# Query, key and value rows of two blocks made inside the first expert stage of a macaron transformer block

## What is computed

```python
x = L0_attn_batch                       # (16, 512, 128) fp32: 8192 rows of 128
x = x + 0.5 * ffn(layernorm(x))         # 8 experts, top 2 by router, sigmoid gates, plus a shared expert
x = x + attn(layernorm(x))              # per batch of 512 rows: q, k, v; softmax per tile of 128 keys;
                                        # the four tiles' results added and divided by their norms; Wo, bo
x = x + 0.5 * ffn(layernorm(x))
# an expert: (silu(g*x @ w_in[e]) * (g*x @ w_sw[e])) @ w_out[e], 128 -> 256 -> 128
```

## Time and profile before

| | us |
|---|---|
| median of three runs | 915.17 (913.69 to 920.29) |
| profiled execution: its time | 916.05 |
| profiled execution: span | 914.3 |
| stage 1, to about | 205 |
| experts(0), about | 205 to 392 |
| attention, about | 392 to 650 |
| experts(1) and the rest, about | 650 to 914 |

### The profile page before, as it was taken

One profiled execution on the slowest core, in us unless ns is written; L12 is line 12 of the kernel. 1 busy time (PEld: TensorE's weight loads), 2 busy tenths in 40 slices (PEclk: granted clock), 3 DMA queues, 4 the chain that ended last, 5 costly groups with the idle time before them and its releaser, 6 DMA issues.

```text
span 914.3 us, 19543 instructions
## 1 busy us (share of the span) xinstructions
PE 817.6 (89%) x5765; PEld 721.4 (79%) x5765; DVE 674.9 (74%) x2191; ACT 573.6 (63%) x1670; POOL 607.7 (66%) x689
## 2 busy tenths in 40 slices
PE   3696877679998999979999999998799999999998
PEld 3475666579998899945777777777599999999997
DVE  6787865746667888836888899897766667777765
ACT  3422432137776677679989899873267667766662
POOL 3888888877777777730466767667656667666670
PEclk9787978889999999989999999998899999999999
DMA  9711111434355555420011111111443345555433
GB/s 243 207 48 49 46 46 49 91 92 111 100 154 149 157 148 142 124 70 1 24 36 37 40 39 42 36 40 45 88 109 91 83 135 164 166 165 144 141 96 101
DMA packets 114091, 88.02 MB, mean 96 GB/s; under 512 B 14595, under 2 KB 103302, under 8 KB 113990
## 3 DMA queue, kind: packets, MB, share of 16 engines
q1 hardware_dynamic: 95840, 51.09, 22.1%
q0 software_dynamic: 17280, 35.69, 12.0%
q10 hardware_dynamic: 870, 0.01, 0.1%
HBM read 43.68 MB, written 43.04 MB: 95 GB/s over the span
## 4 chain that ended last, share of the span: by engine, by line
PE 50%; POOL 30%; issue 9%; DMA 5%; DVE 3%; ACT 2%; SPq 0%; DVEq 0%; POOLq 0%; ACTq 0%
POOL pairs L463 14%; POOL results L989 10%; PE bank L1119 9%; PE bank L1567 5%; PE bank L1591 5%; PE bank L1095 5%; PE bank L1096 5%; PE bank L1097 5%; POOL pairs L1222 3%; PE bank L1577 3%; POOL PAY L454 3%; PE bank L1104 2%; PE bank L1556 2%; PE bank L1544 2%; DMA Y<-results 1%
## 5 line engine op out<-in xcount | busy, mean ns | idle before, releaser
L989 POOL DMA_INDIRECT results<-YO,XS x142 | 149.9, 1056 | 77.7 <-ACT YO L1052 39.9
L1222 POOL DMA_INDIRECT pairs<-PAY,POS x128 | 137.0, 1071 | 75.8 <-DVE POS L259 37.9
L1095 PE MATMUL bank<-round_b,round_a 128*128 128x256 f32 x568 | 172.6, 304 | 11.7 <-DVE round_a L928 10.6
L989 POOL DMA_INDIRECT results<-XTR x142 | 147.1, 1036 | 49.3 <-issue 40.2
L934 DVE TENSOR_TENSOR big<-bank,big 128x512 f32<-128x512 f32 x158 | 109.1, 690 | 87.8 <-PE bank L1097 85.4
L1097 PE MATMUL bank<-round_b,round_a 128*128 128x256 f32 x568 | 161.0, 283 | 0.0
L1096 PE MATMUL bank<-round_b,round_a 128*128 128x256 f32 x568 | 160.9, 283 | 0.0
L463 POOL DMA_INDIRECT pairs<-PAY,POS x128 | 128.3, 1003 | 40.5 <-issue 19.7
L1119 PE MATMUL bank<-WOE,big 128*128 x1136 | 151.2, 276 | 0.1
L1060 ACT ACTIVATE big<-bank 128x512 f32<-128x512 f32 x158 | 94.7, 599 | 75.1 <-PE bank L1097 75.0
L1119 PEld LDWEIGHTS bank<-WOE,big 128*128 128x128 f32 x1136 | 139.1, 193 | 0.6 <-issue 0.5
(11 more groups left out here) (240 smaller groups left out, 1814.9 us busy)
## 6 DMA issues: line engine op xcount, KB each, us to landing
XTR<-pairs SPq DMA_DIRECT2D x71, 130.0 KB
XS<-pairs SPq DMA_DIRECT2D x71, 130.0 KB
Y<-results SPq DMA_DIRECT2D x64, 128.0 KB
YF<-results SPq DMA_DIRECT2D x64, 128.0 KB
pairs<-PAY,POS POOLq DMA_INDIRECT x256, 2.4
out<-X SPq DMA_DIRECT2D x16, 256.0 KB, 3.0
results<-XTR POOLq DMA_INDIRECT x142, 2.6
results<-YO,XS POOLq DMA_INDIRECT x142, 2.4
```

The costliest lines, as they stand in the source:

```text
L989: pool.indirect_dma_start(results, bass.IndirectOffsetOnAxis(ap=XS[:, u, j, AT_DEST:AT_DEST + 1].bitcast(U32), axis=0), YO[:, u, j, :], No ...
L1095: pe.matmul(ps, wl[:, w], hi, start=True, stop=False)
L1222: pool.indirect_dma_start(pairs, bass.IndirectOffsetOnAxis(ap=POS[:, b % AB, j, c:c + 1], axis=0), PAY[:, b % AB, c, j, :], None).then_inc ...
```

## The change

The list of experts(0) gets two entries (`PREPARED`, ahead of tiles 52 and 58) that are no tiles. At such an entry PE turns the normalised rows of block 0 or 1, ACT copies them to `AXT`, PE makes queries, keys and values in the banks that a tile would have used, and ACT takes them out to `QT`, `KT`, `V`. ACT makes the deviations of blocks 0 to 2 in one go in the step of tile 40, DVE the shifts in the step of tile 42, and ACT normalises half a block in each of the steps of tiles 44 to 47 (blocks 0, 1) and of tiles 61 and 62 (block 2). The attention stage leaves out these steps for these blocks. The buffers concerned are allocated before experts(0) instead of after it.

```diff
+    PRE = 2
+    NORMED = 3
+    NORMED_FROM = 44
+    PREPARED = (52, 58)
...
                 for i in range(NT):
+                    if not ffn and i in PREPARED:
+                        tile_at.append(None)
...
+                def nth(n):
+                    return past + n - prepared_to(n) + 1
+
+                normed_at = {} if ffn else {NORMED_FROM + 2 * b + h: (b, h) for b in range(PRE) for h in range(2)}
+                if not ffn:
+                    normed_at.update({PREPARED[-1] + 3 + h: (PRE, h) for h in range(2)})
...
+                    def shifts():
+                        dve.wait_ge(k["a_rstd"], NORMED)
+                        dve.scalar_tensor_tensor(out=NA[:, 0:NORMED, :], in0=MA[:, 0:NORMED, :, 0], scalar=-1.0,
+                                                 in1=RA[:, 0:NORMED, :], op0=ALU.mult, op1=ALU.mult)\
+                           .then_inc(k["a_shift"], NORMED)
...
+                            if not ffn and t == NORMED_FROM - 2:
+                                shifts()
...
+                    def deviations():
+                        act.preload_act_table_set("natural_log_exp_and_others")
+                        act.wait_ge(k["a_stats"], 2 * NORMED)
+                        act.activation(LA[:, 0:NORMED, :], MA[:, 0:NORMED, :, 1], ACT.Ln, bias=eps_c[:, :])\
+                           .then_inc(k["a_log"], NORMED)
+                        act.wait_ge(k["a_log"], NORMED)
+                        act.activation(RA[:, 0:NORMED, :], LA[:, 0:NORMED, :], ACT.Exp, scale=-0.5)\
+                           .then_inc(k["a_rstd"], NORMED)
+
+                    def normalise_half(b, h):
+                        act.wait_ge(k["a_shift"], NORMED)
+                        if b >= 2:
+                            act.wait_ge(k["a_turned"], b - 1)
+                        for j in range(2 * h, 2 * h + 2):
+                            ins = act.activation(AN[:, b % 2, j, :], X[:, BT * b + j, :], ACT.Identity,
+                                                 bias=NA[:, b % 4, j:j + 1], scale=RA[:, b % 4, j:j + 1])
...
+                    def rows_across(n):
+                        b = block_of(n)
+                        act.wait_ge(k["a_turned"], b + 1)
+                        act.activation(AXT[:, b, :], bank[2 + n % 2][:, :], ACT.Copy).then_inc(k["a_copied"], 1)
+
+                    def take_across(n):
+                        b = block_of(n)
+                        act.wait_ge(k["q_made"], b + 1)
+                        act.activation(QT[:, b, :], bank[2 + n % 2][:, :], ACT.Identity, bias=bq_s[:, :], scale=SCALE)\
+                           .then_inc(k["q_ready"], 1)
...
+                            if n >= 2 and is_prep(n - 2):
+                                pe.wait_ge(k["k_ready"] if g else k["q_ready"], prepared_to(n - 2))
...
+                    def turn_rows(n):
+                        b = block_of(n)
+                        pe.wait_ge(k["a_normed"], b + 1)
+                        pe.wait_ge(k["e_silu"], nth(n - 2))
+                        for j in range(BT):
+                            mm = pe.transpose(chunk(bank[2 + n % 2], j), AN[:, b, j, :], ident[:, :])
+                        mm.then_inc(k["a_turned"], 1)
+
+                    def make_rows(n):
+                        b = block_of(n)
+                        pe.wait_ge(k["a_copied"], b + 1)
+                        pe.matmul(bank[2 + n % 2][:, :], WT[:, 0, :], AXT[:, b, :], start=True, stop=True)\
+                          .then_inc(k["q_made"], 1)
+                        pe.wait_ge(k["e_hid"], nth(n - 2))
+                        pe.matmul(bank[4 + n % 2][:, :], WT[:, 1, :], AXT[:, b, :], start=True, stop=True)\
+                          .then_inc(k["k_made"], 1)
+                        pe.wait_ge(k["e_out"], tile_at[n - 2] + 1)
...
+                            if is_prep(i):
+                                turn_rows(i)
+                            else:
+                                up(i)
...
+                        if 0 <= i - 1 < ALL and is_prep(i - 1):
+                            make_rows(i - 1)
+                        elif 0 <= i - 1 < ALL:
                             down(i - 1)
...
-                    if 0 <= i + 3 < NB:
+                    if NORMED <= i + 3 < NB:
                         shift(i + 3)
...
-                    if 0 <= i + 2 < NB:
+                    if PRE <= i + 2 < NB:
                         turn(i + 2)
```

More of the change, by code:

```diff
@@ L862, in is_half, with is_prep, is_tile, prepared_to @@
                 def is_half(n):
-                    return tile_at[n] is None
+                    return ffn == 1 and tile_at[n] is None
+                def is_prep(n):
+                    return ffn == 0 and tile_at[n] is None
+                def is_tile(n):
+                    return tile_at[n] is not None
+                def prepared_to(n):
+                    return tile_at[:n + 1].count(None) if ffn == 0 else 0
+                def block_of(n):
+                    return prepared_to(n) - 1
+                def nth(n):
[3 more added lines that the diff above has]
+                    normed_at.update({PREPARED[-1] + 3 + h: (PRE, h) for h in range(2)})
+                    assert NORMED_FROM > sum_place(NORMED - 1) + 8 and NORMED_FROM + 2 * PRE < PREPARED[0]
                 def halves_to(n):
@@ L970, in _ @@
                                 dve_moments(dve, st, *halved_at[t])
-                        if i + 3 < ALL and not is_half(i + 3):
+                        if i + 3 < ALL and is_tile(i + 3):
                             no.ahead(tile_at[i + 3])
                         if i + 2 < ALL:
-                            low(i + 2)
-                            if i + 2 and not is_half(i + 2):
+                            if not is_prep(i + 2):
+                                low(i + 2)
+                            if i + 2 and is_tile(i + 2):
                                 weights(i + 2)
@@ L1064, in _ @@
                         if i + 2 < ALL:
-                            high(i + 2)
+                            if not is_prep(i + 2):
+                                high(i + 2)
                         elif ffn and i < ALL:
@@ L1069, in _ @@
                             scale(tile_at[i + 3], 1)
-                        if 0 <= i - 1 < ALL and not is_half(i - 1):
+                        if 0 <= i - 1 < ALL and is_tile(i - 1):
                             send(i - 1)
+                        elif 0 <= i - 1 < ALL and is_prep(i - 1):
+                            take_across(i - 1)
+                        if not ffn and 0 <= i < ALL and tile_at[i] == NORMED_FROM - 4:
+                            deviations()
+                        if 0 <= i < ALL and tile_at[i] in normed_at:
+                            normalise_half(*normed_at[tile_at[i]])
                 @block.tensor
@@ L1122, in down @@
                         mm.then_inc(k["e_down"], 1)
+                    def turn_rows(n):
[14 more added lines that the diff above has]
+                        pe.wait_ge(k["e_out"], tile_at[n - 2] + 1)
+                        pe.matmul(bank[6 + n % 2][:, :].rearrange("p (j d) -> p j d", d=D), ones[0:3, :],
+                                  bias3[:, 0:1, :].to_broadcast([3, BT, D]), start=True, stop=False)
+                        for j in range(BT):
+                            mm = pe.matmul(chunk(bank[6 + n % 2], j), AXT[:, b, j * P:(j + 1) * P], WT[:, 2, :],
+                                           start=False, stop=(j == BT - 1))
+                        mm.then_inc(k["v_made"], 1)
                     no.ahead(0)
```

92 lines of the change are left out of this document (51 added, 41 removed).

## The result

The changed kernel is slower: 923.65 us against 918.29 us (medians of 14 runs each, taken in turn), a ratio of 1.0075 with a 95% interval of 1.0057 to 1.0092, so 6.9 us (5.2 to 8.4); the two medians by themselves lie 5.4 apart.

The account below looks back on a forecast made before the run. TensorE was taken to bound the expert tiles, with POOL just as near the edge, and ACT attention's first blocks. Cost 5.3 + 0.3 = 5.6, gain 3.4 + 0.5 = 3.9: 1.7 us slower, 916.9 us from 915.17; range 909.5 to 921.5.

Parts of the forecast that it names:

- terms of the start: Start of attention: scores follow the last tile at once, maximum(0, 1) waits for Y of block 15; gain 3.4 us (3.2 to 4.2).
- the cost of the entries: Tiles 49 to 70: two entries add 7.14 us of TensorE, partly refilling 2.1 us of idling; 5.3 us taken (5.0 to 7.1).
- T at 399 or later: Sign of a wrong forecast: TensorE's last tile ends (T) at 399 us or later, not near 397; entries cost more than their matmuls.
- eight tiles: After an entry: POOL, needing 2.71 us a tile, fills its lag again within eight tiles (8 x 0.16 = 1.3 us).
- Cost 5.0 to 8.1: Bounds of the whole cost in the sum; with gain 2.9 to 5.7 they gave -0.7 to +5.2 us.
- Deviations and normalising: Tile 40's step and six half blocks: table loads 0.3 us (bounds 0 and 3.1), normalising nothing, 1 us if not.
- the cover named for it: Tile 40's step: DVE's 1.98 us wait for Y of block 5 leaves Silu idle 2.23 us, covering most of 3.1 us.
- After maximum(0, 1): Blocks 0 and 1 of attention: at most 1.5 us less work, 1 to 1.6 lost to half clock; gain 0.5 (-0.3 to 1.5).
- The start gives nothing back: Rival, start of attention: late Y of block 15 and half clock leave gain 2, cost 6 to 7.1; +4 to +5 us; chance 0.17.
- More is hidden: Rival, entries and start: entries refill more idle time, Y lands 1.2 us sooner, clock costs nothing; -2 to -4 us; chance 0.25.
- Table loads at each Identity: Rival, ACT in the expert stage: Silu's set lacks Identity, 14 us reach TensorE, some 930 us; chance 0.04.

Follow-up runs that it names:

- e2: Changed kernel with total and added of blocks 14 and 15 moved later in DVE's attention queue (i == 4 and 6): ratio 0.9925 to the kernel before.
- e1: Changed kernel with its second entry ahead of tile 60 instead of 58: ratio 1.0062 to the kernel before.
- e4: Changed kernel with ten extra useless 512-column matmuls on TensorE while it waits for exps(0, 1): ratio 1.0049 to the kernel before.
- e8: Changed kernel with every total(b) and what follows it one tile's step later in the first expert stage: ratio 0.9999 to the kernel before.
- e10: Kernel before, with every total(b) one tile's step later in its first expert stage: ratio 0.9967 to the kernel before.
- e12: Kernel before, totals one tile's step later in the first expert stage and the last totals late in attention: ratio 0.9931 to the kernel before.
- e9: Changed kernel, totals one tile's step later in the first expert stage and the last totals late in attention: ratio 0.9849 to the kernel before.

## Why the prediction was wrong, point by point

**The sign and most terms of the start were right.** The scores follow the last tile at once, Y of block 15 takes the place of the rows as the last thing, maximum(0, 1) comes 11.7 us after the last send instead of 15.2: a gain of 3.5 for the 3.4 forecast. e2 showed the mechanism.

**The step that failed is the cost of the entries**, "I take 5.3", bounded by "if none, 7.1". It measured 8.6 us (7.9 to 8.8 between any two of the executions at full clock, 65.4 to 65.8 less 57.0 to 57.4), and the sign named for it, T at 399 or later, was met: 398.9 in an execution that was 2.2 us ahead at tile 36. The forecast counted TensorE's idle time, 2.1 us, as room that entries fill; the windows show it grown from 1.94 to 3.65 us, beside 6.9 us of added work. Blocks 9 and 11 did lose their waits. But past each entry TensorE ran up to the totals of blocks 10, 12 and 13 at its own pace again and waited there. The upper bound left out that waits can grow. One reason stands in the sum itself: POOL was to need eight tiles to fall behind again by its 1.3 us. Timeline of POOL, changed kernel: its first DMAs for tiles 52 (the first behind an entry) and 53 (which completes the rows of block 10):

```profile
348.69 1.36 POOL L1025 DMA_INDIRECT results<-XTR  x1 [3.31 <-ACT XTR L1088]
...
352.18 0.97 POOL L1025 DMA_INDIRECT results<-XTR  x1 [0.30 <-issue]
```

The outputs of these tiles were out at 348.4 and 351.0: POOL's lag went from 0.3 to 1.2 us in a single tile, and it was 1.3 at tile 53 in the kernel before. So nothing was left for block 10 of what POOL had caught up; e1, e2 and e4 have the same 1.2 us.

e8 shows the cause by moving nothing but the totals and what hangs on them: TensorE idles 0.7 us, and the stretch takes 62.3 us. That is 5.3 more than the kernel before, the forecast's own number, but partly by luck: against e10 and e12, which have the same move and no entries, e8 and e9 give 4.6 to 5.5. The mistake was to leave the totals' places, set by hand for a list without entries, out of the sum.

Why Y of block 13 came later in relation to its tile (wait 2.43, in e1, e2 and e4 2.5 to 3.2) is open. POOL's lag at tile 65, which completes these rows, was only about 0.4 us larger; the rest lies between POOL's second DMA for that tile and SP's last fetch for the block (2.5 us before, 4.1 after), and no run separates what takes this time.

**The upper end of the sum was also added up wrongly.** "Cost 5.0 to 8.1" is less than its own bounds give, 7.1 for the entries and 3.1 for the table loads.

**Deviations and normalising**, 0.3 forecast, measured 0.6 within a scatter that is larger. The number holds, but not by the cover named for it. In the changed kernel DVE did not wait for Y of block 5. The two table loads put the outputs of tiles 40 to 42 about as late as that wait had done before: from the send of tile 39 to that of tile 43 it is 12.0 us, 12.1 before. The loads took the place of the wait rather than passing under it.

**After maximum(0, 1)** the forecast had 0.5 us of gain (-0.3 to 1.5); it was a loss of 1.0 (25.5 instead of 24.5 to value(2)). Two terms share the miss. At full clock (e4, 23.7) the work taken away is worth 0.8 us where up to 1.5 was counted, and the clock costs 1.8 us by e4, for 1 to 1.6. Throttled by default, released by activity, as the Trainium skill has it (TensorE: Matmul & The Clock Gate, What's actually happening): this trace agrees, with 0.50 for 8 us of sparse matmuls after 9.2 us of none.

**The rivals.** "The start gives nothing back" (+4 to +5) was nearest in size. Its gain of 2 at the start is nearer to the measured 2.5 than the forecast's 3.9, and the slow clock was half of its reason; Y of block 15, the other half, landed at T + 10.3 and not at T + 11.5. Its cost of 6 to 7.1 fell short like the forecast's. "More is hidden" was wrong. Table loads at each Identity didn't come; identity under Silu's table needs none, as the Trainium skill says (ScalarE: Activation LUTs, Table sets: the hidden batching unit). The misses, 3.3 us for the entries, 0.3 for the preparation and 1.5 after maximum(0, 1), make up the 5.1 us between 1.7 and 6.8. The rest of the distance between the forecast time, 916.9, and the measured 923.65 is the kernel before, whose median came out at 918.29 beside the changed one, and not at 915.17.

## What to carry to other kernels

Work put into a stretch where two engines stand at their limit and meet at a wait whose place was set by hand can cost its own time and what the wait then adds: move the wait's place with it, or bound the cost above the work's own time. When a start is brought forward, look in every queue for what stands ahead of the first instruction of the new path and when its data land; here moving two additions was worth twice the change's loss. And measure such a change together with the moves that it calls for: alone it lost 0.75%, with them it is part of a gain of 1.5%, of which the moves alone, without it, give 0.7% (e12).

## What was not expected of the hardware

Four 512-column matmuls (two scores) that took 1.88 us took 3.75 at a granted clock of 0.50. The clock had fallen while TensorE had nothing to do for 9.19 us, and it stayed there until about 420, with TensorE busy 6.34 us of the 8 from 412 to 420. Before the change it had been 0.50 from 396 to about 402.
